# Expert units of 256 rows in place of 128 in a fused attention and mixture-of-experts kernel

## What is computed

```python
mod = (silu(c) @ wmod).reshape(32, 6, 1, 128)        # sa, ca, ga, sb, cb, gb
h = layernorm(x) * (1 + ca) + sa
x = x + ga * attention(h)                             # 16 heads, rms norm of q and k, gate, Wo
h = layernorm(x) * (1 + cb) + sb
rw = softmax(h @ router_w.T)                          # 8192 tokens x 32 experts
vals, idx = top_k(rw, 2)
for e in range(32):                                   # only the two chosen experts count
    acc = acc + h * w_masked[:, e:e+1] @ expert_weights[e]
x = x + gb * acc
```

## Time and profile before

| | us |
|---|---|
| median of 3 runs (lowest, highest) | 1106.03 (1105.79, 1109.98) |
| profiled execution | 1105.79 |
| its span, first to last instruction | 1104.0 |
| busy: DVE, PE, POOL, ACT | 729.7, 671.1, 540.8, 531.6 |

### The profile page before, as it was taken

One profiled execution on the slowest core, in us unless ns is written; L12 is line 12 of the kernel. 1 busy time (PEld: TensorE's weight loads), 2 busy tenths in 40 slices (PEclk: granted clock), 3 DMA queues, 4 the chain that ended last, 5 costly groups with the idle time before them and its releaser, 6 DMA issues. The chain is left out here.

```text
span 1104.0 us, 25129 instructions
## 1 busy us (share of the span) xinstructions
PE 671.1 (61%) x5746; PEld 432.2 (39%) x5747; DVE 729.7 (66%) x2237; ACT 531.6 (48%) x1326; POOL 540.8 (49%) x884
## 2 busy tenths in 40 slices
PE   2465788878788788888887887886157660000000
PEld 0133454555454455555554544553156650000000
DVE  5474778889889888988898898973322642233333
ACT  1234667667677767767776777765112220000000
POOL 4121235555565655555556656655600007567665
PEclk9978989999999988999999999998568895555555
DMA  2236555544444443445345444422057773333333
GB/s 57 64 86 170 120 134 149 135 123 118 127 111 119 116 120 101 124 106 134 103 115 125 113 121 116 116 80 64 29 143 209 205 209 83 102 93 99 107 97 98
DMA packets 142594, 128.15 MB, mean 116 GB/s; under 512 B 17748, under 2 KB 126004, under 8 KB 142548
## 3 DMA queue, kind: packets, MB, share of 16 engines
q1 hardware_dynamic: 112020, 96.01, 33.8%
q0 software_dynamic: 8192, 16.79, 5.5%
q10 hardware_dynamic: 22336, 14.82, 4.5%
HBM read 76.52 MB, written 50.46 MB: 115 GB/s over the span
## 5 line engine op out<-in xcount | busy, mean ns | idle before, releaser
L1106 DVE TENSOR_REDUCE negmax<-mx_ps 128x2 f32<-128x512 f32 x512 | 340.7, 684 | 94.7 <-PE mx_ps L1457 53.3
L862 ACT ACTIVATE pr<-st_ps 128x512 f32<-128x512 f32 x512 | 286.7, 597 | 55.6 <-PE st_ps L1479 49.1
L1457 PE MATMUL mx_ps<-k_aug,q_aug 126*128 126x256 bf16 x1024 | 205.0, 285 | 92.2 <-DVE negmax L1106 58.3
L746 POOL DMA_INDIRECT yg<-ys_d,gi x128 | 124.6, 973 | 176.6 <-DMA ys_d<-ys 116.3
L1479 PE MATMUL st_ps<-q_aug,k_aug 128*128 128x256 bf16 x1024 | 177.8, 283 | 0.5 <-ACT pr L862 0.4
L1493 PE MATMUL o_ps<-pr,v_aug 128*32 128x256 f32 x2048 | 141.9, 395 | 44.3 <-issue 25.9
L707 POOL DMA_INDIRECT xs_d<-h,slot x128 | 127.7, 998 | 55.9 <-DVE slot L1229 31.9
L1457 PEld LDWEIGHTS mx_ps<-k_aug,q_aug 126*128 126x128 bf16 x1024 | 78.3, 100 | 194.1 <-issue 185.4
L1479 PEld LDWEIGHTS st_ps<-q_aug,k_aug 128*128 128x128 bf16 x1024 | 97.9, 104 | 35.3 <-issue 11.4
L1493 PEld LDWEIGHTS o_ps<-pr,v_aug 128*32 128x32 f32 x2048 | 56.8, 111 | 94.8 <-issue 74.8
L1359 DVE TENSOR_SCALAR yw<-yg,p_all 128x128 f32<-128x128 f32 x64 | 16.4, 308 | 113.0 <-DMA yg<-ys_d,gi 82.2
(11 more groups left out here) (166 smaller groups left out, 1245.3 us busy)
## 6 DMA issues: line engine op xcount, KB each, us to landing
q_aug<-q_d SPq DMA_DIRECT2D x64, 192.0 KB
xs<-xs_d SPq DMA_DIRECT2D x160, 64.0 KB, 2.0
ys_d<-ys ACTq DMA_DIRECT2D x40, 256.0 KB, 2.6
mod_o<-mod_d SPq DMA_DIRECT2D x32, 256.0 KB
bias_p<-bias_d SPq DMA_DIRECT2D x32, 200.0 KB
q_d<-parts SPq DMA_DIRECT2D x32, 192.0 KB, 2.1
k_d<-parts SPq DMA_DIRECT2D x32, 192.0 KB, 2.1
k_aug<-k_d SPq DMA_DIRECT2D x64, 96.0 KB
```

What stands on the lines that cost most here:

```text
L746: nc.gpsimd.indirect_dma_start(yg[:, par, k, :], None, ys_d, bass.IndirectOffsetOnAxis(ap=gi[:, par, k:k + 1], axis=0)).then_inc(yg_ld[par ...
L862: nc.scalar.activation(pr[:, h % PR], st_ps[score_bank(b, h)][:], ACT.Exp, scale=SCALE).then_inc(exp_d, 1)
L1106: v.tensor_reduce(negmax[:, :, h], mx_ps[h % 2][:], AX.X, ALU.max, negate=True).then_inc(mx_d, 1)
L1457: last = t_.matmul(mx_ps[h % 2][:, qc], q_aug[b.par][0:MROW, h, qc * P:(qc + 1) * P], k_aug[b.par][0:MROW, h, :], start=True, stop=True)
```

## The change

The unit becomes 256 rows, and a group two units. Derived sizes follow:

| | before | after |
|---|---|---|
| UR, UG (rows of a unit, units of a group) | 128, 4 | 256, 2 |
| UNITS, GROUPS_E (units, groups) | 160, 40 | 96, 48 |
| turns of the loop over four groups | 10 | 12 |
| loads of rows (SP), stores of results (ACT) | 160, 40 | 96, 48 |
| zeros written, in 8 transfers | 4 MB | 8 MB |
| table columns, PE transposes of it | 512, 4 | 256, 2 |

A unit's rows are dealt to partitions two at a time (row 2p and 2p + 1 on partition p), so a run of 1024 bytes is contiguous in DRAM, where before it was 512. The result is stored in the same layout. Before, the table needed two columns of 128 units; now it fits in one.

```diff
-UR = P
+UR = 2 * P
-UG = 4
+UG = 2
-LOAD = 8
-TABLE_STEPS = 9
+TABLE_STEPS = 10
-        zeros = sb("zeros", [P, 8 * P])
+        zeros = sb("zeros", [P, 2 * 8 * P])
-            regs = []
-            for k in range(0, UG * XB, LOAD):
-                start = n * (UG * XB) + (lo + k)
...
+            start = n * (UG * XB) + lo
+            cols = table[0:1, start:start + UG * XB] if isinstance(start, int) else table[0:1, bass.ds(start, UG * XB)]
             for k in range(UG):
-                eng.dma_start(xs_sb[i][:, k, :], xs_d[bass.ds(rows[i * UG + k], UR), :]).then_inc(xs_ld[i], 16)
+                eng.dma_start(xs_sb[i][:, k * TB:(k + 1) * TB, :],
+                              xs_d[bass.ds(rows[i * UG + k], UR), :].rearrange("(p k) f -> p k f", k=TB)).then_inc(xs_ld[i], 16)
-                    act.dma_start(empty.rearrange("e (a k) f -> e a (k f)", k=8), zeros[:]).then_inc(lead_st, 16)
+                    act.dma_start(empty.rearrange("e (a k) f -> e a (k f)", k=16), zeros[:]).then_inc(lead_st, 16)
-                act.dma_start(ys_d[g * UG * UR:(g + 1) * UG * UR, :].rearrange("(u p) f -> p u f", u=UG),
-                              ys_sb[i][:]).then_inc(ys_st[i], 16)
+                act.dma_start(ys_d[g * UG * UR:(g + 1) * UG * UR, :].rearrange("(u p k) f -> p u k f", u=UG, k=TB),
+                              ys_sb[i][:].rearrange("p (u k) f -> p u k f", u=UG)).then_inc(ys_st[i], 16)
-            for k in range(2):
-                ins = v.tensor_scalar(uge[:, k], ubeg[:], iota_p[:, k:k + 1], None, ALU.is_le)
-            chained(ins)
+            chained(v.tensor_scalar(uge[:], ubeg[:], iota_p[:, 0:1], None, ALU.is_le))
-            v.tensor_copy(table[0:1, :], o_ps[0:1, 0:4 * P]).then_inc(table_d, 1)
+            v.tensor_copy(table[0:1, :], o_ps[0:1, 0:2 * P]).then_inc(table_d, 1)
-            for k in range(4):
+            for k in range(2):
                 last = t_.matmul(o_ps[0:1, k * P:(k + 1) * P], ucol[:, k:k + 1], ident[:], start=True, stop=True)
-                                     we[:, bass.ds(cols[i * UG + k], P)], start=True, stop=True)
+                                     we[:, bass.ds(cols[i * UG + k // TB], P)], start=True, stop=True)
```

More of the change, by code:

```diff
@@ L59 @@
 TG = UG * UR // P
-assert P < UNITS <= 2 * P and REGION % UR == 0 and (UNITS - LEAST) % 8 == 0
+assert UNITS <= P and REGION % UR == 0 and (UNITS - LEAST) % 8 == 0
 LN_EPS, RMS_EPS = 1e-5, 1e-6
 SCALE = float(HD) ** -0.5
-TABLE_STEPS = 9
+TABLE_STEPS = 10
 PR = 8
@@ L108, in build @@
         iota_e = sb("iota_e", [P, E])
-        iota_p = sb("iota_p", [P, 2])
-        iota_u = sb("iota_u", [P, 2])
+        iota_p = sb("iota_p", [P, 1])
+        iota_u = sb("iota_u", [P, 1])
         iota_c = sb("iota_c", [P, E])
@@ L216, in build @@
         ufirst = sb("ufirst", [P, E])
[L217 to L221, removed]
+        uge = sb("uge", [P, E])
+        uin = sb("uin", [P, E])
+        usel = sb("usel", [P, 2, E])
+        ucol = sb("ucol", [P, 2])
+        table = sb("table", [P, 2 * P], I32)
         xs_sb = [sb(f"xs{i}", [P, TG, P]) for i in range(XB)]
@@ L368, in group_rows @@
         def group_rows(engine, n, lo, most):
-            regs = []
-            for k in range(0, UG * XB, LOAD):
-                start = n * (UG * XB) + (lo + k)
[L373 to L377, removed]
+            start = n * (UG * XB) + lo
+            cols = table[0:1, start:start + UG * XB] if isinstance(start, int) else table[0:1, bass.ds(start, UG * XB)]
+            return nc.values_load_multi_w_load_instructions(cols, engines=[engine], min_val=0, max_val=most,
+                                                            skip_runtime_bounds_check_because="the table holds rows and columns of whole units only")[1]
         def load_group(eng, rows, i):
             for k in range(UG):
-                eng.dma_start(xs_sb[i][:, k, :], xs_d[bass.ds(rows[i * UG + k], UR), :]).then_inc(xs_ld[i], 16)
+                eng.dma_start(xs_sb[i][:, k * TB:(k + 1) * TB, :],
+                              xs_d[bass.ds(rows[i * UG + k], UR), :].rearrange("(p k) f -> p k f", k=TB)).then_inc(xs_ld[i], 16)
         def rows_complete(eng):
@@ L549, in _ @@
             for dst, pattern, mult in (
-                (iota_e, [[1, E]], 0), (iota_p, [[P, 2]], 1), (iota_c, [[P, E]], 0), (iota_u, [[P * UR, 2]], UR), (unit0, [[REGION // UR, E]], 0), (carry, [[REGION, E]], 0),
+                (iota_e, [[1, E]], 0), (iota_p, [[1, 1]], 1), (iota_c, [[P, E]], 0), (iota_u, [[UR, 1]], UR), (unit0, [[REGION // UR, E]], 0), (carry, [[REGION, E]], 0),
             ):
@@ L1303, in _ @@
             chained(v.scalar_tensor_tensor(ufirst[:], uend[:], -float(UR), carry[:], ALU.mult, ALU.add))
-            for k in range(2):
-                ins = v.tensor_scalar(uge[:, k], ubeg[:], iota_p[:, k:k + 1], None, ALU.is_le)
-            chained(ins)
[L1307 to L1312, removed]
+            chained(v.tensor_scalar(uge[:], ubeg[:], iota_p[:, 0:1], None, ALU.is_le))
+            chained(v.scalar_tensor_tensor(uin[:], uend[:], iota_p[:, 0:1], uge[:], ALU.is_gt, ALU.mult))
+            v.scalar_tensor_tensor(usel[:, 0], ufirst[:], float(LEAST * UR - IDLE), uin[:], ALU.add, ALU.mult)
+            chained(v.tensor_tensor(usel[:, 1], iota_c[:], uin[:], ALU.mult))
             chained(v.tensor_reduce(ucol[:], usel[:], AX.X, ALU.add))
-            v.tensor_tensor(ucol[:, 0:2], ucol[:, 0:2], iota_u[:], ALU.add).then_inc(tab, 1)
+            chained(v.tensor_tensor(ucol[:, 0:1], ucol[:, 0:1], iota_u[:], ALU.add))
             assert steps[0] == TABLE_STEPS
             dve.wait_ge(tab_ps, 1)
-            v.tensor_copy(table[0:1, :], o_ps[0:1, 0:4 * P]).then_inc(table_d, 1)
+            v.tensor_copy(table[0:1, :], o_ps[0:1, 0:2 * P]).then_inc(table_d, 1)
             nlook = [0]
@@ L1607, in _ @@
             run(pe, step, seed)
-            pe.wait_ge(tab, TABLE_STEPS + 1)
-            for k in range(4):
+            pe.wait_ge(tab, TABLE_STEPS)
+            for k in range(2):
                 last = t_.matmul(o_ps[0:1, k * P:(k + 1) * P], ucol[:, k:k + 1], ident[:], start=True, stop=True)
@@ L1632, in expert_out @@
                     last = t_.matmul(out_bank[i][:, k * P:(k + 1) * P], xsT[i][:, k * P:(k + 1) * P],
-                                     we[:, bass.ds(cols[i * UG + k], P)], start=True, stop=True)
+                                     we[:, bass.ds(cols[i * UG + k // TB], P)], start=True, stop=True)
                 last.then_inc(ye_ps, 1)
             expert_in(0, 0, 0)
-            cols = group_rows(mybir.EngineType.PE, 0, 2 * P, (E - 1) * P)
+            cols = group_rows(mybir.EngineType.PE, 0, P, (E - 1) * P)
             for i in range(XB):
@@ L1642, in _ @@
             with pe.Fori(1, GROUPS_E // XB - 1) as n:
-                cols = group_rows(mybir.EngineType.PE, n, 2 * P, (E - 1) * P)
+                cols = group_rows(mybir.EngineType.PE, n, P, (E - 1) * P)
                 for i in range(XB):
@@ L1647, in _ @@
             last = GROUPS_E // XB - 1
-            cols = group_rows(mybir.EngineType.PE, last, 2 * P, (E - 1) * P)
+            cols = group_rows(mybir.EngineType.PE, last, P, (E - 1) * P)
             for i in range(XB):
```

## The result

The changed kernel took 1114.03 us (median of 13 runs, 1108.85 to 1123.18), the kernel before 1107.13 (13 runs, 1105.15 to 1113.23): a ratio of 1.0064, with a 95% interval of 1.0037 to 1.0093. It is some 7 us slower (4 to 10), where 2.5 us faster was forecast.

What follows compares the result with a forecast made beforehand. SP's issuing of loads was taken to set the expert stage's pace. From 1105.8 us, -18.5 for the expert stage and +16 for the zeros gave 1103.3 us, range 1092 to 1116.

Steps and rivals of the forecast that it cites:

- Part 2: First eight steps of the attention stage: the doubled zeros delay the parts' landing and PE's loads, about +16 us.
- SP's gap: Attention steps with zeros: SP's time from k_d to q_aug should be near 10 us, where it was 6.85.
- PE's waits up to 235: Attention stage: PE's waits for k_aug up to 235 us should grow from 27 us to about 43.
- The start of the expert stage: Expert stage: table made 2.4 us sooner, first load at 801.3, first result 6.9 us after it.
- ACT's ring: Expert stage: ACT's two store buffers are the next limit, 1.65 us a group with stores landing in 2.6.
- the gain of 18.5: Whole expert stage: last result at 891.1 in place of 909.65, 18.5 us sooner.
- Rival 3: Expert stage gains 8 us or none: full DMA engines, ring at 2.0 a group, or PE at half clock; chance 0.10.
- rivals 1 and 2: Attention stage zeros: 1, cheap, +8 or less, chance 0.24; 2, dear, +26, and it ends slower, chance 0.14.
- The DMA price: Expert stage: runs of 1024 bytes move at 348 GB/s, which gives 1.51 us a group.
- A term at nothing: Expert stage: PE's limit was put at 1.33 us a group at full clock.
- Rival 4: Expert stage: 1024-byte runs move as 512, 1.84 us a group, gain 14; chance inside the forecast's 0.52.

Runs made afterwards that it cites:

- the second run: The changed kernel once more, with no edit, as a control and for a second profile: 1122.0 us, 1.0033 to the kernel before.

## Why the prediction was wrong

**Part 2 was right.** +16 was forecast; the first scatter moved by 15.6 and 15.3 us, the first one behind all zeros by 17.1 and 16.7, and the large zeros alone cost 8.5 to 17.5 us. The named signs came: SP's gap "near 10 us" is 10.1, PE's waits up to 235, "about 43", are 42.9. The Trainium skill's rule in "DMA: Bandwidth & Descriptors", "Why a DMA increments its semaphore by 16 and not by 1", that the slowest dimension sets how many engines carry a transfer, is borne out by cause and not only by agreement: 16 in place of 8 in that dimension changed the slices of the DMA view and took 13.4 us from the first scatter. The three stores of `q_d`, issued from 58.7 on, before the first packet of the zeros moves at 60.9, landed in 2.1 us and less; that of `k_d`, issued 0.7 us behind the start of the zeros' issue (59.5), in 10.1, and in 2.1 in the version that issues the zeros at the head of the step, at 47.6. The Trainium skill's rule that a semaphore write lands only after every earlier write of its DMA engine ("DMA: Bandwidth & Descriptors", "Queues, rings and completion order") agrees with these times, but it is not needed for them: the data of `k_d` are late themselves.

The landing of `q_d` (L450) and of `k_d` (L453) in that step:

```profile
L450 SPq DMA_DIRECT2D q_d<-parts x3: 383/490/492, 58.7 to 59.7; - x3
...
DMA to landing us min/median/max: 1.8/2.1/2.1
...
L453 SPq DMA_DIRECT2D k_d<-parts x1: 457/457/457, 60.2 to 60.2; - x1
...
DMA to landing us min/median/max: 10.1/10.1/10.1
```

What SP's queue moves in 65 to 70.3 us, with the zeros on 8 engines (packets, MB, share of 16 engines):

```profile
q1 hardware_dynamic: 200, 0.10, 6.2%
```

And with the zeros on 16 engines, in 64.3 to 67.1 us:

```profile
q1 hardware_dynamic: 400, 0.20, 24.6%
```

The store of `k_d` is 192 KB, 384 packets of 512 bytes and 16 that tell of the landing, and SP issued nothing else behind it. On 8 engines half of these 400 packets move only when most of the zeros are through, on 16 engines all of them do: SP's queue moves none from 61.5 to 64.5. So each engine that carries zeros holds its share of the small store behind them.

**The start of the expert stage was right.** The table came 2.2 us sooner (last scatter to first load 9.3, now 7.1), forecast 2.4; the first result followed the first load after 831.14 - 823.74 = 7.4, forecast 6.9; the gather followed the last result after 3.5, forecast 3.58.

**The step that failed is ACT's ring.** It was named as the limit, and it is. It was sized with a store that lands in 2.6 us, read where SP fed the DMA engines 208 GB/s. When SP no longer holds the loads back, loads and stores together run at 266 GB/s, and the stores land in 3.0 to 3.2 us. The sentence "stores will land no sooner than before" left out that they would land later. The formula itself holds within 0.1 us: (0.7 + 3.2) / 2 = 1.95, measured 1.98; in the second run of this kernel (0.7 + 3.0) / 2 = 1.85, measured 1.95; (0.7 + 3.3) / 2 = 2.0, measured 2.0; (0.7 + 2.3) / 2 = 1.50, measured 1.49; and with the shortest landing and no load beside it (0.7 + 2.1) / 2 = 1.4, measured 1.39 at the stage's end. From the first result to the last I had 3.8 us for two intervals and 79.1 for 45, in all 82.9; it took 93.2. Those 10.3 us and 0.7 at the start turn the gain of 18.5 into 7.6 (9.5 in the second run). That is nearly the whole error: -7.6 in place of -18.5, with +17.1 in place of +16, gives +9.5 in place of -2.5.

**Rival 3 had the number and half of the reason.** It had the ring at 2.0 with stores that land in 3.3 us, time 1114 to 1122, and got a chance of 0.10. I held two things against it. Runs of 1024 bytes are cheaper: true, and of little worth while the ring is the bound. The granted clock is 1: true, and beside the point. It was right to have the range reach it, and wrong to weigh it below rivals 1 and 2, since its own evidence stood in the earlier trace rows: the same store that lands in 2.2 us at best took 3.9 at worst, at a DMA share of 0.73 that the change was bound to raise. Its reason, that loads and stores together *fill* the engines, is not what happened with two buffers (0.85 busy). They are nearly full only with three.

**The DMA price was a little low.** 348 GB/s was read from a stretch with output stores alone. With loads and stores mixed and the engines 0.99 busy they moved 318, so 1.65 us a group and not 1.51. With three buffers the stage then runs a little faster than I had forecast it for two: 1.66 a group, and 23 us less from last scatter to gather where 18.5 was forecast.

**A term at nothing, on PE.** The prediction has PE at "1.33 a group at full clock" and leaves out that PE, like SP, reads the table at each turn of its loop. With the ring of two this hardly showed, since stores released ACT 42 times in 48. With four buffers it makes PE's pace 1.63 a group and not 1.33, so PE stands beside the DMA engines as the next limit.

**Rival 4** (runs of 1024 bytes moved as 512) is false as a mechanism: 0.85 busy in place of 0.92 at the same rate. **Rivals 1 and 2** both priced the zeros wrongly, by 9 us too little and 9 too much.

**Still open.** Why moving the zeros to the head of ACT's step gains twice what was expected was not taken apart: PE's waits fell by 21 us and the first scatter by 18.6, and part of it may be that ACT's own queue was held by the issue. How the loads delay a store in the expert stage (a place in a queue, or the memory) was not separated either; only that their bytes do it. With three buffers or more, PE's turns and the DMA engines were not told apart.

## What to carry to other kernels

When an issuer stops being the bound, the next limit is not to be sized with latencies read while it was: it had held the traffic back, and with it the landing of everything else. A ring of N buffers can run no faster than (work + landing) / N, so a change that shortens the cycle ahead of it should be tried together with one buffer more. Here the third buffer turned a ratio of 1.0033 into 0.993. With the zeros spread and moved it became 0.9642, and 0.982 of that the kernel before reaches by the zeros alone. And a large fill that nothing waits for is paid by the small stores issued right behind it: spread it over all engines and issue it where no such store follows.

## What the runs showed of the hardware that was not expected

The same kernel before took 1041.49 us (20 runs) on one chip and 1109.35 and 1118.67 on another. The difference lies in stages that no experiment touches: 577.8 us from first to last scatter against 627.9, and 174.6 us in the gather against 190.8. Windows from 240 to 700 of the profile before, and of the kernel with a third buffer on the other chip:

```profile
240.00:700.00 460.00, 381.97 (x3503) 237.64 (x3501) 401.03 (x1285) 335.93 (x854) 271.14 (x490) 0.96 0.45 116
```

```profile
240.00:700.00 460.00, 401.78 (x3836) 242.59 (x3836) 437.42 (x1386) 366.09 (x923) 290.53 (x537) 1.00 0.48 125
```

The granted clock of TensorE was 0.96 and 1.00, and in the same time every engine did 8 to 10% more instructions, VectorE 1386 for 1285, more than the 4% of the clock. The cause stays open. A small difference is therefore to be judged by ratios on one chip, and by stages that the change touches, not by the spans of two profiles.
